# Eight pairs of sequences through two loops: the next pair is loaded and normed inside the current pass

## The reference, cut to what matters

```
x = x + L0_attn(ln(x))   # starts with an RMS norm of its own; linear attention, then an MLP
x = x + L0_ffn(ln(x))    # a channel mix
x = x + L1_attn(ln(x))   # causal softmax attention
x = x + L1_ffn(ln(x))    # 2 groups x 32 experts, the 2 best of each group for every token
x = x + L2_attn(ln(x))   # causal softmax attention with rope
x = x + L2_ffn(ln(x))    # 8 experts, the best 2
x = x + L3_attn(ln(x))   # a mamba (state space) layer
x = x + L3_ffn(ln(x))    # attention over heads, then 8 gated experts
```

## Time and profile before

| | us |
|---|---|
| median of 3 runs | 5831.26 (5829.92 to 5835.9) |
| profiled execution | 5804.77 |
| its span | 5803.2 |
| PE busy in the span | 4503.4 (78%) |
| DVE busy | 3665.5 (63%) |
| POOL busy | 2279.9 (39%) |
| ACT busy | 1757.0 (30%) |

### The profile page before, as it was taken

The page is one execution under the profiler, slowest core; times in us unless marked ns, Lnnn a source line. Parts: engine busy times, 40 slices in busy tenths (PEclk is TensorE's granted clock), DMA queues, the critical chain, the costliest instruction groups (busy, mean ns, idle before and its releaser), DMA issues. The chain is left out here.

```text
span 5803.2 us, 89650 instructions
## 1 busy us (share of the span) xinstructions
PE 4503.4 (78%) x33608; PEld 2606.0 (45%) x33608; DVE 3665.5 (63%) x10873; ACT 1757.0 (30%) x2749; POOL 2279.9 (39%) x2754
## 2 busy tenths in 40 slices
PE   5979788797979795958778688787786786877872
PEld 4454445454544443634535435445354354453442
DVE  4565656565656563647586685676765956757665
ACT  2424243333333342423232241232322422413220
POOL 3333333333342334445253271362533623614435
PEclk9989899898989897968888888888888888888885
DMA  3000000000000004720000000000000000000000
GB/s 119 8 16 12 13 13 13 15 11 16 10 20 6 19 7 159 231 72 2 16 14 5 18 8 10 21 2 16 14 5 16 10 9 20 4 13 17 5 14 4
DMA packets 141739, 145.74 MB, mean 25 GB/s; under 512 B 31112, under 2 KB 126026, under 8 KB 140770
## 3 DMA queue, kind: packets, MB, share of 16 engines
q1 hardware_dynamic: 114130, 93.01, 5.5%
q0 software_dynamic: 18432, 37.79, 2.3%
q10 hardware_dynamic: 8736, 8.91, 0.5%
HBM read 69.17 MB, written 62.59 MB: 23 GB/s over the span
## 5 line engine op out<-in xcount | busy, mean ns | idle before, releaser
L815 DVE CUSTOM_DVE_ANT_0 twin<-twin,w_mask_row 128x512 f32<-128x512 f32 (+3 forms) x2048 | 951.5, 522 | 335.4 <-PE twin L1777 333.9
L1777 PE MATMUL twin<-arena 32*128 32x128 f32 (+3 forms) x4096 | 803.5, 519 | 38.9 <-DMA arena<-hres 16.7
L1795 PE MATMUL twin<-arena 32*128 32x128 f32 (+3 forms) x4096 | 792.6, 505 | 33.7 <-DVE arena L815 32.1
L1723 PE MATMUL twin<-w_ident_b 128*128 128x512 bf16 x1536 | 455.1, 449 | 390.3 <-DVE mv L775 158.6
L1450 ACT ACTIVATE arena<-twin 128x768 f32<-128x768 f32 (+1 forms) x544 | 479.3, 881 | 686.6 <-PE twin L1806 387.5
L705 POOL TENSOR_SCALAR ve<-mv 128x4 f32<-128x4 f32 x128 | 27.5, 214 | 1458.9 <-DVE mv L775 1458.3
L1795 PEld LDWEIGHTS twin<-arena 32*128 32x128 f32 x4096 | 348.3, 199 | 479.4 <-issue 289.2
L328 POOL DMA_INDIRECT got<-sorted_y,back x288 | 280.8, 975 | 540.4 <-ACT ring L1657 290.5
L1723 PEld LDWEIGHTS twin<-w_ident_b 128*128 128x128 bf16 x1536 | 155.9, 111 | 660.3 <-DVE mv L775 182.1
L1777 PEld LDWEIGHTS twin<-arena 32*128 32x128 f32 x4096 | 356.9, 206 | 198.1 <-issue 111.2
L320 POOL DMA_INDIRECT sorted_x<-got,w_mo_first_slots x288 | 287.0, 997 | 97.9 <-issue 56.0
(11 more groups left out here) (422 smaller groups left out, 9473.4 us busy)
## 6 DMA issues: line engine op xcount, KB each, us to landing
sorted_y<-arena SPq DMA_DIRECT2D x96, 256.0 KB, 2.8
sorted_x<-zeros ACTq DMA_DIRECT2D x2, 4096.0 KB, 19.9
a<-sorted_x SPq DMA_DIRECT2D x64, 128.0 KB
b<-sorted_x SPq DMA_DIRECT2D x64, 128.0 KB, 2.5
hres<-sorted_x SPq DMA_DIRECT2D x64, 128.0 KB
sorted_x<-got,w_mo_first_slots POOLq DMA_INDIRECT x288
got<-sorted_y,back POOLq DMA_INDIRECT x288, 2.6
x_out<-w_l_w SPq DMA_DIRECT2D x18, 256.0 KB, 2.3
```

The source lines that it names most:

```text
L815: last = dve.tensor_tensor_reduce(s[:, e, at:at + w], s[:, e, at:at + w], W["mask_row"][:, T - w:T], -1.0, 3e38, ALU.add, ALU.min, into)
L1723: pe.matmul(into, ident_b, ident_b.unsqueeze(1).broadcast_to([P, NT, P]), start=True, stop=True, skip_group_check=True)
L1777: last = pe.matmul(s[:, e, at:at + w], queries[r, P * i:P * (i + 1)], keys[r, 0:w], start=(at == 0), stop=True, skip_group_check=True)
L1795: last = pe.matmul(s[:, e, at:at + w], keys[r, P * m:P * (m + 1)], queries[r, P * m:T], start=(at == 0), stop=(tag == "l2"), skip_group_ch ...
```

## The change

Loop 1: `X` of the next pair is loaded during `l1_route`, as soon as the current one is stored and normed. VectorE puts the layer norm and the RMS norm of the next pair between the steps of routing, so a pass begins with the turn of `B`. For the first pair, setup does it all. The input has one more pair at its end (a copy of the first), which the last pass loads and norms for nothing. Loop 2: a new tensor `XN` takes the next pair's x, loaded after the attention. `add_chosen` adds the fetched rows into it in `l3_mamba` and `l3_front`, followed by the layer norm. ScalarE's fills (`clear_rows`) move into `l3_front`. For the first pair the experts' block does it. GpSimd's fetches are moved so that all are issued before the third norm of `l3_mamba`. In both loops the `keep_busy` matmuls at the head are gone.

```diff
@@ setup @@
+                for q in PAIR:
+                    sp.dma_start(X[q][:], x_in[0, q].rearrange("(t p) d -> p t d", p=P)).then_inc(setup["x_loaded"], 16)
                 for name in loaded_first:
...
@@ helpers @@
+        def add_chosen(dve, sg, q, steps):
+            for c in steps:
+                k, g = divmod(c, GROUPS)
+                if c == 0:
+                    dve.wait_ge(sg[f"x_loaded{q}"], 16)
+                    dve.wait_ge(sg[f"m_got{q}"], 16 * SLOTS_OF_SEQ)
+                else:
+                    dve.wait_ge(sg[f"m_adding{q}"], c)
+                for t in range(NT):
+                    n = NT * GROUPS * k + GROUPS * t + g
+                    i = dve.scalar_tensor_tensor(XN[q][:, t], got[q][:, n],
+                                                 back[:, q, SLOTS_OF_SEQ + n:SLOTS_OF_SEQ + n + 1], XN[q][:, t],
+                                                 ALU.mult, ALU.add)
+                i.then_inc(sg[f"m_adding{q}"], 1)
...
@@ sync, loop 1 @@
+                            for q in PAIR:
+                                src = x_in[bass.ds(pair + 1, 1), q].rearrange("b (t p) d -> p (b t) d", p=P)
+                                sp.wait_ge(sg[f"m_kept{q}"], 16)
+                                sp.wait_ge(sg["m_a"], q + 1)
+                                sp.dma_start(X[q][:], src).then_inc(sg[f"x_loaded{q}"], 16)
@@ gpsimd, l3_mamba @@
                                     for m in range(4 * len(PAIR)):
                                         pool.wait_ge(sg["l3_xc"], m + 1)
-                                        fetch_rows(pool, sg, (4 + m,))
+                                        fetch_rows(pool, sg, (4 + 2 * m, 5 + 2 * m))
                                     for m in range(NT * len(PAIR)):
                                         pool.wait_ge(sg["l3_decay"], m + 1)
-                                        fetch_rows(pool, sg, (12 + 2 * m, 13 + 2 * m))
+                                        fetch_rows(pool, sg, (20 + 2 * m, 21 + 2 * m) if m < 4 else (24 + m,))
@@ vector, l1_route @@
+                            for q in PAIR:
+                                dve.wait_ge(sg[f"x_loaded{q}"], 16)
+                                layernorm_stats(q)
                             choose(0)
+                            next_rows(0)          # layer norm into A, squares and sums
                             choose(1)
+                            next_rows(1)
                             place(0)
+                            rms_apply(0, A[0], B[0], "l0_b")
                             place(1)
+                            rms_apply(1, A[1], B[1], "l0_b")
@@ vector, end of loop 2 @@
                             for q in PAIR:
                                 rms_apply(q, ma_y[q], ma_y[q], "l3_y")
+                            add_chosen(dve, sg, 0, range(0, ADDS - 1))
...
+                            add_chosen(dve, sg, 0, range(ADDS - 1, ADDS))
+                            layernorm_stats(0, XN)
+                            add_chosen(dve, sg, 1, range(0, 2))
+                            take_queries(0)
+                            layernorm_apply(0, "l2_a", src=XN)
+                            add_chosen(dve, sg, 1, range(2, ADDS))
+                            layernorm_stats(1, XN)
+                            take_queries(1)
+                            layernorm_apply(1, "l2_a", src=XN)
@@ scalar, l3_front @@
+                            for q in PAIR:
+                                act.wait_ge(sg["l3_out_mm"], q + 1)
+                                clear_rows(act, q)
@@ tensor, heads of the loops @@
-                            keep_busy(pb(0, 0), ("stats_ready", 2), ("stats_ready", 3), ("stats_ready", 4))
...
-                            keep_busy(pb(0, 3), ("m_added", 1), ("stats_ready", 1), ("m_added", 2), ("stats_ready", 2))
```

More of the change, by code:

```diff
@@ L142, in _ @@
             def _(pool):
-                pool.memset(minus_half[:], -0.5)
+                pool.memset(minus_half[:], -0.5).then_inc(setup["half"], 1)
+                pool.wait_ge(setup["half"], 1)
+                for n in range(2 * len(PAIR)):
+                    q = n % len(PAIR)
+                    pool.wait_ge(setup["stats"], n + 1)
+                    if n < len(PAIR):
+                        pool.tensor_scalar(VE[q][:], MV[q][:, :, 1], 1.0, 1e-5, ALU.mult, ALU.add
+                                           ).then_inc(setup["var_eps"], 1)
+                    else:
+                        pool.tensor_scalar(VE[q][:], SSQ[q][:], 1.0 / D, 1e-6, ALU.mult, ALU.add
+                                           ).then_inc(setup["var_eps"], 1)
+                    pool.wait_ge(setup["var_eps"], n + 1)
+                    pool.tensor_tensor(RS[q][:], VE[q][:], minus_half[:], ALU.pow).then_inc(setup["rstd"], 1)
                 pool.memset(zeros[:], 0.0).then_inc(setup["zeros"], 1)
@@ L466, in _ @@
                                                ).then_inc(sg["e_silu"], 1)
+                        act.wait_ge(sg["e_w"], 2 * UNITS)
+                        for i in range(3):
+                            act.wait_ge(sg[f"e_stored{i}"], 16 * (UNITS // 3))
+                        for q in PAIR:
+                            clear_rows(act, q)
                     @block.vector
@@ L555, in _ @@
                     def _(sp):
[L556 to L559, removed]
                         if first <= L1_EXPERTS < last:
@@ L587, in _ @@
                                                      ).then_inc(sg[f"l2_rows{q}{g}"], 16)
+                        for q in PAIR if first <= L2_ATTENTION < last else ():
+                            src = kept_x[bass.ds(pair + 2, 1), q].rearrange("b (t p) d -> p (b t) d", p=P)
+                            sp.wait_ge(sg["l2_moved"], q + 1)
+                            sp.dma_start(XN[q][:], src).then_inc(sg[f"x_loaded{q}"], 16)
                         for q in PAIR if last >= LAYERS else ():
@@ L1726, in turn @@
                         def turn(q, src, wait, n, ready, b=0):
-                            pe.wait_ge(sg[wait], n)
+                            if wait:
+                                pe.wait_ge(sg[wait], n)
                             for t in range(NT):
```

201 lines of the change are left out of this document (113 added, 88 removed).

## The result

| | us | ratio to before, 95% interval |
|---|---|---|
| before, median of 4 runs | 5830.59 (5825.0 to 5835.9) | |
| changed, median of 4 runs | 5766.6 (5757.67 to 5776.85) | 0.9889 (0.9869 to 0.9909) |
| changed, on a second chip, 6 runs | 5713.47, before there 5786.8 | 0.9871 (0.9843 to 0.9898) |
| profiled execution of changed | 5775.45, span 5773.9, clock 0.853 | |

The change gains 64 us in the first comparison and 73 in the second. I had forecast 104 and 5727 us: the sign and the range were right, but the gain that I forecast was 1.4 to 1.6 times the measured one.

A forecast was written before the change was run, and what follows sets the result against it. Each pass's head, a chain of latencies with nothing beside it, was the bound attacked, TensorE being busiest at 78%. Loop 1's 22.6 us and loop 2's 81.6 made 104 off 5831.3: 5727 us, range 5697 to 5783.

The forecast's parts named there:

- The step that failed: Head of loop 1's pass: transposes come first, `F` at about 1.4 us instead of 13.5, saving 12.1 us a pass.
- Tail of loop 1: Routing in loop 1: two stats, two norms and one scaling added in full on VectorE, 8.2 us a pass.
- Experts' block: Before loop 2: adds, stats, power and norm of the second sequence follow its landing, 8.4 us later, once.
- First pass: Start of loop 1: 16.5 us of head go, two more DMAs delay the weights by 1.0; 15.5 us saved.
- Loop 2's tail: End of loop 2's pass: 3.0 us added; twelve adds hidden with 0.5 to spare, ScalarE's fills done in time.
- Clock: Heads without filling matmuls: transposes and first projections run at half rate, costing 1.5 us a pass in loop 1, 2.0 in loop 2.
- The other reading that the prediction gives: Activity releases the clock: only half of one set of transposes is charged, 0.6 us a pass in each loop, total 18 us better.
- Clock low for ten us after the start: Rival, both loops: 5 us a pass in place of 1.5 and 2.0, 52 us back, 5779 us; chance 0.14.
- Transfers late: Rival: loop 1's load of `X` lands late, VectorE stands 4.0 us every routing, 32 us in all, 5759 us; chance 0.13.
- Linear attention at half rate: Slower rival, loop 1: TensorE's linear attention takes 70 us instead of 35, 280 us in eight passes, 6007 us; chance 0.05.
- Does less than it says: A shrunken head could uncover another wait, such as 2.01 us before the first scores; given no case of its own.
- The base: Timed runs' median lies 26.5 us above the profiled execution of 5804.8, so 104 us were taken off 5831.3.

The follow-up runs named there:

- experiments 11 and 10: One profiled execution each on one chip: the kernel before, 5843.73 us (11), and the changed kernel, 5761.73 us (10).
- experiment 1: The changed kernel with a prefetch hint on the branch that closes each loop: 5667.62 us against 5793.31 before, ratio 0.9784.
- experiment 2: The kernel before with the same prefetch hint on the loops' branch: ratio 0.9998 to the kernel before.
- the experiments on the sends: The changed kernel with GpSimd's 16 sends of rows moved from the linear into the softmax attention: 0.9863, again 0.9889; with the prefetch hint too 0.9828.
- experiment 8: The changed kernel with the prefetch hint and 24 filling matmuls in TensorE's idle time at the end of loop 1's routing: 5667.31 us, ratio 0.9797.

## Why the prediction was right, and where it was too high

Measured on one chip (experiments 11 and 10), in the terms of the sum, us a pass where nothing else stands:

| term | forecast | measured |
|---|---|---|
| loop 1: `F` after the table load | 1.4 | 4.4 to 5.1 |
| loop 1: head, clock included | -10.6 | 17.5 to 10.1: -7.5 |
| loop 1: tail | +8.2 | 18.65 to 26.71: +8.1 |
| first pass, to keys and values, once | -14.0 | 69.42 to 55.82: -13.6 |
| experts' block, once | +8.4 | 316.4 to 324.8: +8.4 |
| loop 2: to the first scores | -14.25 | 26.0 to 14.3: -11.7 |
| loop 2: tail | +3.0 | 11.3 to 14.7: +3.4 |
| loop 2: period | -11.25 | 389.0 to 380.3: -8.7 |
| total | -104 | -82, and -64 and -73 in the timed runs |

Times their counts the measured rows come to about -62 us. The other 20 of the 82 lie in stages of loop 1 that the change doesn't touch (8 of them in the linear attention) and are the scatter of two single executions.

- **The step that failed** is the first of the change: "the transposes are TensorE's first work of the pass [...] So `F` comes at about 1.4 us". I counted what each engine has to do and wait for, and not the branch that TensorE takes to get there. It moved `F` from 1.4 to 4.4 to 5.1 us, 3.0 to 3.7 at each of 14 starts, 44 us in all, and the missing gain is 104 - 62 = 42; experiment 1 gave about 50 of it back, experiment 2 shows that only the change laid it bare. I had dismissed a head that "could uncover another wait" since what came to mind hangs on `F`; this one stands ahead of `F`. The Trainium skill (Runtime: NRT & Kernel Launch, "Instruction fetch mechanics") says that a taken branch to code outside the engine's window waits for a DMA of its page. TensorE's 3.4 us agree, with the packet of instructions inside each long branch, and so does the cure by a hint; I had not weighed that page.
- **The range** held partly by luck: its upper part, to 5783, was made for a clock that stays low, which did not come; the branch, which had no term, filled it.
- **Tail of loop 1**: right, and to 0.1 us. **Experts' block**: right. **First pass**: right to 0.4, since no branch leads there.
- **Loop 2's tail**: 3.4 for 3.0. The twelve adds are hidden with 0.60 us to spare (0.5 forecast), GpSimd's powers are no longer behind fetches, the fills of ScalarE are done (the last begins at 3323.30 with 1.89 us) before its copy at 3328.52.
- **Clock**: from `F` to the first scores of loop 2 it is in most passes 9.7 us for 8.5, so 1.2 in place of 2.0; in loop 1 `F` to keys and values grew by 0.7 to 1.5 us in the first profile and by 1.4 to 1.8 in experiment 10, forecast 1.5. The other reading that the prediction gives, 0.6 us a pass, is too low. The clock stood at 0.50 until 878.1, 7.3 us into the pass and not 3 to 5, since TensorE began 3.6 us late. Two sets of transposes and the first projections ran at 0.50, the second pair of projections (878.13, 1.12 us for two) at full rate.
- **Rivals.** Clock low for ten us after the start: no. Transfers late: no, landings took 3.1 to 3.5 us in loop 1. Linear attention at half rate: no; over the 40 us behind 886 in the first profile the clock was 0.96 on average (windows below), but on the chip of experiments 10 and 11 it stood at 0.54 for ten of these us, in both kernels alike, so it doesn't bear on the difference. "Does less than it says", to which I gave no case, is what happened.

```profile
886.00:926.00 40.00, 36.90 (x559) 29.26 (x556) 26.37 (x29) 8.84 (x20) 24.67 (x20) 0.96 0.09 28
```

- **The base** was soft as well: the profiled execution of before was of the kind with the short linear attention and 26.5 us under the median. I carried that over as a constant, and nothing shows that both came from one chip.

Fastest was the change with the hint: 0.9784, that is 126 us under before on its chip. With the fill in the routing it is the same.

## What to carry to other kernels

Before the head of a loop is made short, look at the line of the loop itself, engine by engine: a long branch costs nothing as long as something else is late, and is the next bound when it is not. Where work moves out of a head into a tail in which that engine has no idle time, only the wait is won: in loop 1, with the hint, the early load paid, the moved norms did not. And before a difference between two profiles is explained, see whether stages that the change doesn't touch moved too; here they moved with the chip, in both kernels, and one more run of the same kernel would have shown it before the experiments on the sends.

## What the runs showed of the hardware

- TensorE's branch back over a pass took 3.3 to 5.1 us without a hint and 0.34 to 0.39 with one; VectorE's, ScalarE's, GpSimd's and SyncE's took 0.04 to 0.08 without. In one kernel (experiment 2) the hinted branch took 3.4 to 4.1 us at four starts of loop 2 and 0.46 to 1.09 at three.
- In the changed kernel each long branch holds a 16 KB packet of an instruction queue, 0.93 to 1.44 us long; the short ones (experiment 1) hold none.
- One chip of the four in the experiments was slower in a stage of dense small matmuls (32 rows, 128 columns): 35 against 86 started in 3.5 us at a granted clock of 1.00, and 44 against 35 us for the stage.
- A clock that had been brought to 1.00 ahead of a pass (experiment 8) stood there while TensorE was idle for 3.4 us, fell to 0.50 just after it began again, and came back 3.4 us later, with TensorE 3.18 of 3.2 us busy in between.
